# The start of a layer of two blocks: who normalizes, when the first conv tiles are projected, where the gate products stand

## The reference, cut to what matters

```python
x = x + _L0_attn_ref(_layernorm(x), ...)      # (x - mean) / sqrt(var + 1e-5), per row
# inside:
proj = einsum('bld,pd->blp', hidden_states, in_proj_w)
gate, hbc, dt = proj[..., :I], proj[..., I:I + CONV_DIM], proj[..., -H:]
conv = conv_bias + sum(pad[:, k:k + L, :] * conv_weight[:, k] for k in range(4))
xBC = silu(conv)                              # x, B, C of the scan
dt_p = softplus(dt + dt_bias);  dA = exp(dt_p * -exp(A_log))
# scan over the 1024 rows, + x * D, group norm, * silu(gate), out_proj
```

## Time and profile before

| | us |
|---|---|
| median of three runs | 1302.47 |
| the profiled execution | 1304.97 |
| its span | 1303.2 |
| PE busy in the span | 1232.2 (95%) |
| DVE / ACT / POOL busy | 938.0 / 693.6 / 654.6 |
| PE busy in 0 to 10, 10 to 20 and 20 to 30 us | 2.05, 4.72, 9.19 |

### The profile page before, as it was taken

One profiled execution on the slowest core, in us unless ns is written; L12 is line 12 of the kernel. 1 busy time (PEld: TensorE's weight loads), 2 busy tenths in 40 slices (PEclk: granted clock), 3 DMA queues, 4 the chain that ended last, 5 costly groups with the idle time before them and its releaser, 6 DMA issues.

```text
span 1303.2 us, 21987 instructions
## 1 busy us (share of the span) xinstructions
PE 1232.2 (95%) x6680; PEld 970.7 (74%) x6690; DVE 938.0 (72%) x1734; ACT 693.6 (53%) x1042; POOL 654.6 (50%) x707
## 2 busy tenths in 40 slices
PE   5999999999999999999999999999679999889976
PEld 4777777787778778777777877777567777667754
DVE  5786778669668866966876696688756555469995
ACT  3676676567567666756666666665313333222210
POOL 5057546655655655565465566545633343433330
PEclk9999999999999999999999999999879999889996
DMA  5111021011102101100200120000103222211100
GB/s 177 46 51 34 2 67 34 19 34 49 33 1 65 33 17 33 58 24 1 74 24 17 33 65 17 23 16 2 40 17 113 97 85 89 87 54 44 48 17 25
DMA packets 44234, 57.52 MB, mean 44 GB/s; under 512 B 10118, under 2 KB 21160, under 8 KB 43930
## 3 DMA queue, kind: packets, MB, share of 16 engines
q1 hardware_dynamic: 44185, 56.92, 14.5%
HBM read 49.95 MB, written 6.96 MB: 44 GB/s over the span
## 4 chain that ended last, share of the span: by engine, by line
PE 81%; DVE 7%; issue 5%; POOL 4%; ACT 2%; DMA 1%; SPq 1%; POOLq 0%; DVEq 0%; ACTq 0%
PE p_tile L94 13%; PE p_d L94 9%; PE p_gate L94 9%; PE p_tile L98 6%; PE p_y L1123 4%; PE p_d L98 4%; PE p_in L1102 4%; PE p_gate L98 4%; PE p_x L1110 4%; PE t_p_a L1878 2%; PE p_d L1082 2%; PE p_x L1059 2%; PE p_y L94 2%; PE t_p_c L1946 1%; PE p_gb L94 1%
## 5 line engine op out<-in xcount | busy, mean ns | idle before, releaser
L705 DVE SCALAR_TENSOR_TENSOR conv<-p_tile,conv_taps,conv 128x511 f32<-128x511 f32 x189 | 141.3, 748 | 51.4 <-ACT conv L582 36.3
L815 DVE TENSOR_TENSOR em<-em,p_gb 128x512 f32<-128x512 f32 x128 | 82.1, 682 | 66.6 <-ACT em L616 66.5
L525 POOL TENSOR_TENSOR squares<-squares 128x256 f32<-128x256 f32 x64 | 47.2, 738 | 131.5 <-ACT squares L640 131.5
L94 PE MATMUL p_tile<-xn_hi,wc_hi 128*128 128x512 f32 x252 | 110.7, 439 | 0.8 <-DVE halo L709 0.8
L640 ACT ACTIVATE squares<-y 128x512 f32<-128x512 f32 x64 | 40.4, 632 | 123.4 <-DVE y L849 122.4
L705 DVE SCALAR_TENSOR_TENSOR conv<-p_gate,conv_taps,conv 128x511 f32<-128x511 f32 (+2 forms) x90 | 67.0, 745 | 46.7 <-ACT conv L582 43.0
L94 PE MATMUL p_tile<-xn_lo,wc_hi 128*128 128x512 f32 x252 | 98.7, 392 | 0.0
L94 PE MATMUL p_d<-wr_hi,zt_hi 128*128 128x512 f32 x236 | 93.9, 398 | 1.5 <-ACT em L616 1.5
L495 POOL TENSOR_TENSOR x_w<-xs,head_g 128x512 f32<-128x512 f32 x56 | 58.8, 1049 | 68.5 <-ACT xs L612 63.5
L94 PE MATMUL p_d<-wr_lo,zt_hi 128*128 128x512 f32 x236 | 93.0, 394 | 0.0
L587 ACT ACTIVATE xbc<-conv 128x512 f32<-128x512 f32 x96 | 60.7, 632 | 59.6 <-DVE conv L713 37.3
(11 more groups left out here) (388 smaller groups left out, 3622.5 us busy)
## 6 DMA issues: line engine op xcount, KB each, us to landing
w_raw<-w SPq DMA_DIRECT2D x108, 256.0 KB, 2.7
q_words<-q SPq DMA_DIRECT2D x33, 256.0 KB, 2.6
h_ring<-h_lo_rows SPq DMA_DIRECT2D x6, 704.0 KB, 4.7
h_lo_rows<-h_rest SPq DMA_DIRECT2D x11, 256.0 KB, 2.1
x_res<-x SPq DMA_DIRECT2D x8, 256.0 KB, 4.6
out<-out_t SPq DMA_DIRECT2D x8, 256.0 KB, 2.2
h_lo_rows<-h_rest SPq DMA_DIRECT2D x11, 128.0 KB, 1.9
gate_second<-w SPq DMA_DIRECT2D x4, 256.0 KB, 5.0
```

Source lines behind the costliest of these rows:

```text
L94: pe.matmul(out, lhs(k)[0], rhs(k)[n], start=(start and k == 0 and n == 0), stop=False)
L705: ve.scalar_tensor_tensor(out=conv[:, s, sh:], in0=p[:, 0:HALF - sh], scalar=conv_w[:, bass.ds(g, 1), j, tap], in1=conv[:, s, sh:], op0=AL ...
L815: ve.tensor_tensor(m, m, gm.unsqueeze(1).broadcast_to([P, HG // 2, P]), ALU.mult)\
```

## The change

It touches the prologue alone, on all five engines.

- **Normalizing.** ACT writes the normalized tile (`ln_norm`: Identity with scale rstd and bias -mean*rstd). DVE instead makes the bias, a 128x1 operation that overwrites the mean. On ACT the list is norm 0, norm 1, round 0, norm 2, round 1, and so on.
- **dt's weights.** ACT rounds w_dt (after tile 3), POOL takes the rest (after the eighth power); POOL sets the mask at the start. DVE loses all four.
- **Banks.** The conv tiles use `FIRST_BANK`: p_tile, p_d1, p_in, p_x, p_tile, p_d1, and tile j waits for the taps of tile j - 4.
- **PE's order.** Before: conv 0, conv 1, gate 0, gate 1, dt's transposes, gate 2, conv 2 to 5, gate 3. After: conv 0 to 3, gate 0, dt's transposes, conv 4, conv 5, gate 1, gate 2, gate 3. Gate 1 and gate 2 (p_in, p_x) wait for the taps of conv 2 and conv 3.
- **ACT and DVE in the dt chain.** ACT's tile_in 0 stands before the logarithm, tile_in 1 after the last exponential; DVE's taps of tile 0 stand inside the dt chain (before L931's step), those of tile 1 after it. The gate silus move later.
- **SP.** Five loads (head_rows, and d_lhs and d_rhs twice) are issued behind the first ten weights instead of ahead of them.

```diff
+    FIRST_BANK = (p_tile, p_d1, p_in, p_x, p_tile, p_d1)
...
@@ -545,10 +546,15 @@
...
+        pool.memset(t_mask, 1.0).then_inc(s_split_dt, 1)
+        pool.wait_ge(s_split_dt, 1)
+        pool.memset(t_mask[:, 0:HALF:P], 0.0).then_inc(s_split_dt, 1)
         pool.wait_ge(ln_rs, 1)
         for c in range(NC):
-            pool.wait_ge(ln_var, 2 * (c + 1))
+            pool.wait_ge(ln_var, 3 * c + 2)
             pool.tensor_tensor(rstd[:, c:c + 1], rstd[:, c:c + 1], m_half[:], ALU.pow).then_inc(ln_rs, 1)
+        pool.wait_ge(dt_ac, 1)
+        pool.tensor_tensor(lo_of(WT - 1), w_dt[:], hi_of(WT - 1).bitcast(F32), ALU.subtract).then_inc(s_split_dt, 1)
...
@@ -645,39 +651,54 @@
...
-        for c in range(NC):
+        def ln_norm(c):
+            act.wait_ge(ln_var, 3 * c + 3)
+            wait(act, ln_tr, c - 1)
+            act.activation(xnt[:, c % 2, :], x_res[:, c, :], ACT.Identity, bias=mean_var[:, c, 0:1],
+                           scale=rstd[:, c:c + 1]).then_inc(ln_xn, 1)
+        def ln_round(c):
             act.wait_ge(ln_tr, c + 1)
             act.activation(xn_hi[:, :, c * P:(c + 1) * P], (p_x, p_in)[c % 2][:].rearrange("p (k t) -> p k t", k=KT),
                            ACT.Copy).then_inc(ln_hi, 1)
-            if c >= CH:
-                w_round(0, c - CH)
+        for c in range(NC + 1):
+            if c < NC:
+                ln_norm(c)
+            if c > 0:
+                ln_round(c - 1)
+            if c == CH:
+                act.wait_ge(s_const, 16 * 6)
+                act.activation(hi_of(WT - 1), w_dt[:], ACT.Copy).then_inc(dt_ac, 1)
+            if c > CH:
+                w_round(0, c - CH - 1)
...
-        act.wait_ge(s_const, 16 * 6)
-        act.wait_ge(dt_ve, 4)
+        act.wait_ge(dt_ve, 2)
         act.activation(t_e, t_v, ACT.Abs).then_inc(dt_ac, 1)
-        act.wait_ge(dt_ac, 1)
+        act.wait_ge(dt_ac, 2)
         act.activation(t_e, t_e, ACT.Exp, scale=-1.0).then_inc(dt_ac, 1)
         act.activation(head_c[:, 3:4], head_c[:, 1:2], ACT.Exp).then_inc(dt_ac, 1)
-        act.wait_ge(dt_ve, 5)
+        tile_in(0, 0, 0, FIRST_BANK[0])
+        act.wait_ge(dt_ve, 3)
         act.activation(t_r, t_w, ACT.Ln).then_inc(dt_ac, 1)
-        act.wait_ge(dt_ac, 4)
+        act.wait_ge(dt_ac, 5)
         act.activation(t_rem, t_r, ACT.Exp, scale=-1.0).then_inc(dt_ac, 1)
-        tile_in(0, 0, 0, p_tile)
-        tile_in(1, 0, 1, p_d1)
-        gate_silu(0, 0, 0)
-        gate_silu(1, 1, 0, p_in)
-        act.wait_ge(dt_tp, 3)
-        act.activation(by_half(dtw_t), transposed(p_gb), ACT.Exp).then_inc(dt_ac, 1)
-        act.activation(by_half(etot_t), transposed(p_d0), ACT.Exp).then_inc(dt_ac, 1)
+        tile_in(1, 0, 1, FIRST_BANK[1])
         for j in range(TILES):
             tile_silu(j, 0, j, 0)
+            if j + 2 < TILES:
+                tile_in(j + 2, 0, j + 2, FIRST_BANK[j + 2])
             if j == 0:
+                gate_silu(0, 0, 0)
+                act.wait_ge(dt_tp, 3)
+                act.activation(by_half(dtw_t), transposed(p_gb), ACT.Exp).then_inc(dt_ac, 1)
+                act.activation(by_half(etot_t), transposed(p_d0), ACT.Exp).then_inc(dt_ac, 1)
+            if j == 3:
+                gate_silu(1, 1, 0, p_in)
+            if j == 4:
                 gate_silu(2, 2, 0, p_x)
-            if j + 2 < TILES:
-                tile_in(j + 2, 0, j + 2, (p_tile, p_d1)[j % 2])
         gate_silu(3, 3, 0)
...
@@ -887,52 +908,41 @@
...
-            if 2 <= c < NC + 2:
-                ve.wait_ge(ln_rs, c)
-                wait(ve, ln_tr, c - 3)
-                ve.tensor_scalar(xnt[:, c % 2, :], x_res[:, c - 2, :], mean_var[:, c - 2, 0:1],
-                                 rstd[:, c - 2:c - 1], ALU.subtract, ALU.mult).then_inc(ln_xn, 1)
+            if 1 <= c <= NC:
+                ve.wait_ge(ln_rs, c + 1)
+                ve.scalar_tensor_tensor(out=mean_var[:, c - 1, 0:1], in0=mean_var[:, c - 1, 0:1], scalar=-1.0,
+                                        in1=rstd[:, c - 1:c], op0=ALU.mult, op1=ALU.mult).then_inc(ln_var, 1)
             if c < NC:
                 ve.wait_ge(ln_st, c + 1)
                 ve.bn_aggr(mean_var[:, c, :], stats[:, c, :]).then_inc(ln_var, 1)
             if 3 <= c:
                 ln_rest(c - 3)
             if c < NC:
-                ve.wait_ge(ln_var, 2 * c + 1)
+                ve.wait_ge(ln_var, 3 * c + 1)
                 ve.tensor_scalar(rstd[:, c:c + 1], mean_var[:, c, 1:2], EPS, None, ALU.add).then_inc(ln_var, 1)
...
-            if c == CH + 1:
-                ve.tensor_copy(hi_of(WT - 1), w_dt[:]).then_inc(dt_ve, 1)
-                ve.memset(t_mask, 1.0).then_inc(dt_ve, 1)
-                ve.wait_ge(dt_ve, 2)
-                ve.tensor_tensor(lo_of(WT - 1), w_dt[:], hi_of(WT - 1).bitcast(F32), ALU.subtract)\
-                    .then_inc(s_split_dt, 1)
-                ve.memset(t_mask[:, 0:HALF:P], 0.0).then_inc(s_split_dt, 1)
+        ve.wait_ge(s_const, 16 * 6)
         for a in range(2):
             rows = slice(a * H, (a + 1) * H)
             ve.wait_ge(dt_mm, a + 1)
             ve.tensor_scalar(t_v[rows], (p_d0, p_d1)[a][rows, :], head_c[rows, 0:1], None, ALU.add)\
                 .then_inc(dt_ve, 1)
...
-        ve.wait_ge(dt_ve, 8)
-        ve.wait_ge(dt_ac, 5)
+        tile_taps(0, 0, 0, 0, range(TAPS), FIRST_BANK[0])
+        ve.wait_ge(dt_ve, 6)
+        ve.wait_ge(dt_ac, 6)
         ve.tensor_tensor(t_dt, t_dt, t_rem, ALU.mult).then_inc(s_split_dt, 1)
...
-        tile_taps(0, 0, 0, 0, range(TAPS), p_tile)
+        tile_taps(1, 0, 1, 0, range(TAPS), FIRST_BANK[1])
...
@@ -980,7 +990,7 @@
             if bank is not None:
-                wait(pe, s_tap, TAPS * (j - 1))
+                wait(pe, s_tap, TAPS * (j - 3))
...
@@ -1136,31 +1146,33 @@
...
         for a in range(2):
             pe.wait_ge(ln_lo, CH * (a + 1))
             three_pass(pe, (p_d0, p_d1)[a][:],
                        lambda k: (k_part(hi_of(WT - 1), k), k_part(lo_of(WT - 1), k)),
                        lambda k: (xn_hi[:, k, half_cols(a)], xn_lo[:, k, half_cols(a)]), KT).then_inc(dt_mm, 1)
-        conv_tile(0, 0, 0, 0, p_tile)
-        pe.wait_ge(dt_ve, 4)
-        conv_tile(1, 0, 1, 0, p_d1)
+        conv_tile(0, 0, 0, 0, FIRST_BANK[0])
+        pe.wait_ge(dt_ve, 2)
+        for j in range(1, CH):
+            conv_tile(j, 0, j, 0, FIRST_BANK[j])
         gate_product(0, 0, 0)
-        gate_product(0, 1, 0, p_in)
-        pe.wait_ge(dt_ve, 11)
+        pe.wait_ge(dt_ve, 9)
...
-        gate_product(0, 2, 0, p_x)
-        for j in range(2, TILES):
-            conv_tile(j, 0, j, 0, (p_tile, p_d1)[j % 2])
+        for j in range(CH, TILES):
+            conv_tile(j, 0, j, 0, FIRST_BANK[j])
+        for j, bank in ((1, p_in), (2, p_x)):
+            pe.wait_ge(s_tap, TAPS * (j + 2))
+            gate_product(0, j, 0, bank)
         pe.wait_ge(s_sg, 1)
         gate_product(0, 3, 0)
...
```

More of the change, by code:

```diff
@@ L362, in sync @@
         sp.dma_start(d_b[:], io["d_rows"]).then_inc(s_const, 16)
[L363 to L366, removed]
         def load_w(g, w):
@@ L396, in sync @@
             load_w(0, w)
+        sp.dma_start(head_rows[:], io["head_rows"]).then_inc(s_dconst, 16)
+        for i in range(2):
+            sp.dma_start(d_lhs[:, i, :], io["d_lhs"]).then_inc(s_dconst, 16)
+            sp.dma_start(d_rhs[:, i, :], io["d_rhs"]).then_inc(s_dconst, 16)
         for k in range(PART):
-            wait(sp, dt_ve, 12 + k)
+            wait(sp, dt_ve, 10 + k)
             for a in range(2):
@@ L900, in vector @@
             if c < NC:
-                ve.wait_ge(ln_var, 2 * c + 1)
+                ve.wait_ge(ln_var, 3 * c + 1)
                 ve.tensor_scalar(rstd[:, c:c + 1], mean_var[:, c, 1:2], EPS, None, ALU.add).then_inc(ln_var, 1)
-            if c == CH:
-                ve.wait_ge(s_const, 16 * 6)
-            if c == CH + 1:
-                ve.tensor_copy(hi_of(WT - 1), w_dt[:]).then_inc(dt_ve, 1)
-                ve.memset(t_mask, 1.0).then_inc(dt_ve, 1)
-                ve.wait_ge(dt_ve, 2)
-                ve.tensor_tensor(lo_of(WT - 1), w_dt[:], hi_of(WT - 1).bitcast(F32), ALU.subtract)\
-                    .then_inc(s_split_dt, 1)
-                ve.memset(t_mask[:, 0:HALF:P], 0.0).then_inc(s_split_dt, 1)
+        ve.wait_ge(s_const, 16 * 6)
         for a in range(2):
@@ L920, in vector @@
                 .then_inc(dt_ve, 1)
-        ve.wait_ge(dt_ac, 2)
+        ve.wait_ge(dt_ac, 3)
         ve.tensor_scalar(t_w, t_e, 1.0, None, ALU.add).then_inc(dt_ve, 1)
-        ve.wait_ge(dt_ve, 5)
+        ve.wait_ge(dt_ve, 3)
         ve.tensor_scalar(t_dt, t_w, -1.0, None, ALU.add).then_inc(dt_ve, 1)
         ve.tensor_scalar(t_v, t_v, 0.0, None, ALU.max).then_inc(dt_ve, 1)
-        ve.wait_ge(dt_ve, 7)
+        ve.wait_ge(dt_ve, 5)
         ve.tensor_tensor(t_dt, t_e, t_dt, ALU.subtract).then_inc(dt_ve, 1)
-        ve.wait_ge(dt_ve, 8)
-        ve.wait_ge(dt_ac, 5)
+        tile_taps(0, 0, 0, 0, range(TAPS), FIRST_BANK[0])
```

(31 more changed lines are left out.)

## The result

The changed kernel is slower. The median of four runs is 1310.7 us (1309.16 to 1311.35), that of the kernel before beside them 1302.45 (1302.17 to 1303.63); the ratio is 1.0055, 95% interval [1.0042, 1.0067]. The profiled execution took 1310.77 us, its span is 1309.0. The forecast was 1296.2.

A forecast was written before the change was run, and what follows sets the result against it. PE was busy for 95% of the span, so time was to be had where PE idles or its work starts late. Terms of 3.2 + 2.15 + 0.95 = 6.3 us off 1302.47 gave 1296.2 us, 8-in-10 range 1294.6 to 1298.7.

The forecast's parts named there:

- the last sentence of the sum: Later stages: group 0 enters with each engine 6.1 to 6.6 us earlier, and all waits from there are relative.
- the only rival on the slower side: Later stages: PE's low clock of 1.2 GHz lasts longer, using up the 6.3 us; 1303 us, chance 0.03.
- what would show the forecast wrong: Listed signs: PE waiting at dt's transposes or for taps, 1.2 GHz over 7 us, or early group 0 with end unmoved.
- Term 1: Layer norm: shorter DVE rounds, so the eighth tile's transposes end at 19.74 instead of 22.92; 3.2 us gained.
- under cover: Prologue: work leaving DVE, such as POOL's rest of w_dt from 17.2 to 18.5, is off the path; cost 0.
- The rival in which it rises at 27.9: dt's first product: PE's clock rises when it did, so the slow stretch is 3.2 longer; 1.6 lost, 1297.8, chance 0.13.
- Terms 2 and 3: PE from conv 0 to group 0: waits for taps (2.14 us) and for tile 5's silu (0.95 us) go.
- The dt chain was late: dt chain: 1.2 us late behind tile_in 0, but covered by PE's products ahead of the transposes with 1.5 to spare.
- The taps did not become the bound: Rival at gate 1: taps wait 0.3 more per tile, PE stops about 1 us in all; 1297.2, chance 0.07.
- The sum: Whole kernel: 3.2 + 2.15 + 0.95 = 6.3 us gained, giving 1296.2 us.

The follow-up runs named there:

- a_w4: The changed kernel with a second, long-met wait on four DVE instructions of the prologue, no instruction added; 1297.47 us, ratio 0.9948 to the kernel before.
- a_ve4_behind: The changed kernel with four one-column memsets on DVE behind the loop; 1309.91 us, ratio 1.0050 to the kernel before.
- a_ve3: The changed kernel with three one-column memsets at the head of DVE's list; 1311.94 us, ratio 1.0056 to the kernel before.
- b_mask_pool: The kernel before with only the mask's two memsets moved from DVE to POOL; 1302.75 us, ratio 0.9994 to the kernel before.
- a_ve4: The changed kernel with four one-column memsets at the head of DVE's list; 1297.21 us, ratio 0.9954 to the kernel before.

## Why the prediction was wrong

**The step that failed** is the last sentence of the sum: "all waits from there on are relative". Group 0 did start some 6.7 us earlier on PE, and a_w4, which has the same prologue but for four waits already met, shows that the loop then takes its 113.0 us a turn. But waits for a semaphore aren't all that an engine waits for. Its list has a place, the change moved DVE's loop from entry 342 to 332, and an edge lay at 336. What the runs showed in place of relative waits: DVE stands 2.36 and 1.97 us for its own list at each of five jumps back, a turn takes 115.4 us instead of 113.0, and 12.5 us come together over the seven groups (803.2 against 790.7 in a_w4). The prediction carried a gain to the end over 790 us of steady state, and the only rival on the slower side was the clock. The case was named among what would show the forecast wrong (group 0 starts early and the end doesn't move), with no mechanism behind it, and I had not counted DVE's list. What there was to see in the profile of before: the page's row of q14 with its 24 packets. It would have told nothing of the nearness of an edge; that needs the list.

**Term 1** was 3.2 and measured 3.47 at conv 0, but by luck: misses of both signs nearly cancel, and one of them belongs to this profile and not to the change. The transposes ended 2.77 earlier, not 3.2: DVE's last 128x1 step took 1.22 instead of the 0.16 of its sisters, beside POOL's rest of w_dt, which I had put "under cover". The rows of POOL and DVE:

```profile
16.85 1.27 POOL L557 TENSOR_TENSOR wr_lo<-e_cum,wr_hi 128x512 fp32r<-128x512 f32 x1
16.92 1.22 DVE L913 SCALAR_TENSOR_TENSOR mean_var<-mean_var,rstd 128x1 f32<-128x1 f32 x1 [0.66 <-POOL rstd L555]
```

Both end at the same time (18.12 and 18.14). Statistics that were to start at 5.51 as before started at 5.81, when their rows of x had landed. Against that the last four rounds were 1.55 us long, not 1.70. The normalization took 0.80 or 0.81, for 0.78. Two of them on ACT:

```profile
10.92 0.81 ACT L657 ACTIVATE em<-x_res,mean_var,rstd 128x512 f32<-128x512 f32 x1 [0.46 <-DVE mean_var L913]
...
12.47 0.81 ACT L657 ACTIVATE em<-x_res,mean_var,rstd 128x512 f32<-128x512 f32 x1 [0.25 <-DVE mean_var L913]
```

The other 0.70 came from the clock: the four L98 matmuls of dt's first half took 1.02 where they had taken 1.71 (26.34 to 28.05), 0.26 instead of 0.43 for 512 columns. The change did not bring that. With the new layer norm these four took from 0.93 (a_ve4_behind, the same prologue) to 1.67 (a_ve3), and with the old one 0.93 in b_mask_pool and 1.71 in the kernel before: how long the slow stretch lasts differs from profile to profile. The rival in which it rises at 27.9 fell, since PE's matmuls went at the pace of 2.4 GHz from about 23.6 on; that the rise may come earlier or later against the work is what the runs show.

**Terms 2 and 3** were 3.10 and measured 3.21: p_gb moved by 6.68, conv 0 by 3.47. From conv 0 to group 0's transposes PE took 28.93 us (27.21 to 56.14) where the prediction had 28.99. The dt chain was late, as worked out, and hidden: the remainders, the last that the transposes wait for, were ready at 39.65 (L955, 38.96 and 0.69), and PE came to them at 40.92 without a wait, with 1.3 to spare for the 1.5 of the prediction. The taps did not become the bound; no row of PE has an idle time in that stretch.

**The sum** of 6.3 is what the change gives once DVE's loop stands in its old relation to the edge: a_w4 at 1297.47 and a_ve4 at 1297.21 against the forecast of 1296.2, with before 1.3 and 1.1 us above its first median in those comparisons. The gain of 0.46 to 0.52% is 6.0 to 6.8 us, with intervals from 4.0 to 8.6. These two are the fastest of the kernels compared in several rounds, and a_w4 needs one line in four places.

## What to carry to other kernels

Where a kernel has a hardware loop, count the entries of the compiled list ahead of it, second waits included, before and after an edit: a loop longer than 256 entries can stand in two or in three pieces of the list, and an edit in code that runs once then moves the cost of every turn. The signs are "issue" idle time at the loop's first instructions, behind every jump back but not at the entry, and more packets in the instruction queue's row; a few entries ahead of the loop are the cure, and an experiment that separates an edit's own worth from that of its place. A forecast that carries a prologue's gain through a loop is to be given a rival for the loop itself.
